# An attention kernel on Trainium2: the normalisation of the rows on ScalarE instead of VectorE

## The reference, cut to what matters

```
mod = (silu(c) @ wmod).reshape(8, 6, 1, 512)       # sa, ca, ga, sb, cb, gb
h = layernorm(x) * (1 + ca) + sa                    # x: 8 x 512 x 512, fp32
x = x + ga * attention(h, W_attn, W_proj)           # 16 heads of 32, causal
h = layernorm(x) * (1 + cb) + sb
x = x + gb * mlp(h)                                 # 512 -> 1024 -> 1024 -> 512
layernorm(x) = (x - mean(x)) / sqrt(var(x) + 1e-5)  # over the last axis
```

## Time and profile before

| | |
|---|---|
| median of 3 runs | 1541.73 us (1539.03 to 1541.76) |
| profiled execution, its own time | 1542.99 us |
| its span, first to last instruction | 1541.2 us |
| mean granted clock of TensorE | 0.973 of full |
| busy in the span: PE / DVE / ACT / POOL | 94% / 72% / 52% / 28% |

### The profile page before, as it was taken

How to read it: one execution, slowest core, us unless ns; L and a number is a source line. 1 busy time by engine, 2 the same in 40 slices (tenths; PEclk the granted TensorE clock), 3 DMA queues, 4 the chain that set the end, 5 groups by cost and what they waited for, 6 DMA issues and landing times.

```text
span 1541.2 us, 30440 instructions
## 1 busy us (share of the span) xinstructions
PE 1449.8 (94%) x12112; PEld 1314.9 (85%) x12112; DVE 1109.9 (72%) x1957; ACT 808.2 (52%) x1462; POOL 439.2 (28%) x451
## 2 busy tenths in 40 slices
PE   7989999999999999995599999998999999999998
PEld 6678878787888888874489999998999999999998
DVE  5377877777777877673577676787766666788887
ACT  3156666667666667674355555566333333353331
POOL 2146665667666766664000000000000000000000
PEclk9889999999999999997799999999999999999999
DMA  6634435244434343442434454363765556688895
GB/s 219 164 85 102 120 84 127 72 121 96 119 82 121 83 123 93 98 98 81 172 126 162 158 176 159 138 213 135 251 234 201 201 210 215 231 295 266 296 304 184
DMA packets 126590, 247.16 MB, mean 160 GB/s; under 512 B 13672, under 2 KB 36200, under 8 KB 126448
## 3 DMA queue, kind: packets, MB, share of 16 engines
q1 hardware_dynamic: 122816, 242.57, 50.5%
q10 hardware_dynamic: 3632, 2.64, 0.5%
HBM read 114.58 MB, written 79.72 MB: 126 GB/s over the span
## 4 chain that ended last, share of the span: by engine, by line
PE 45%; DVE 4%; ACT 2%; DMA 1%; issue 1%; SPq 0%; DVEq 0%; ACTq 0%
PE sum_b L2149 12%; PE sum_e L2149 8%; PE sum_a L2149 8%; PE aux L2089 6%; PE sum_b L2145 4%; PE sum_e L2145 3%; PE sum_a L2145 3%; PE aux L2099 1%; PE aux L2077 1%; DVE w L1841 1%; DVE op L1703 1%; DMA wproj_whole<-wproj_t 1%; ACT u_c L1443 0%; DMA y_dram<-u_c 0%; DMA blk<-y_dram 0%
## 5 line engine op out<-in xcount | busy, mean ns | idle before, releaser
L429 POOL TENSOR_TENSOR prob_lo<-prob,prob_hi 128x512 f16<-128x512 f32 x256 | 296.9, 1165 | 140.8 <-ACT prob L533 140.5
L526 ACT ACTIVATE prob_hi<-key_score 128x512 f16<-128x512 f32 x320 | 191.1, 597 | 130.6 <-PE key_score L824 128.2
L2149 PE MATMUL sum_b<-op,w 128*128 128x256 f32 x1728 | 217.9, 284 | 3.2 <-DVE p_c L1743 1.6
L735 PE MATMUL lin<-h_parts,wqkv 128*128 128x512 f32 x768 | 218.5, 408 | 1.1 <-DVE h_parts L578 1.1
L2149 PEld LDWEIGHTS sum_b<-op,w 128*128 128x128 f32 x1728 | 211.2, 192 | 5.4 <-issue 3.3
L533 ACT ACTIVATE prob<-key_score 128x512 f32<-128x512 f32 x320 | 190.7, 596 | 0.0
L697 DVE TENSOR_REDUCE row_max<-score 128x1 f32<-128x512 f32 (+2 forms) x384 | 180.4, 499 | 12.8 <-PE score L811 12.1
L735 PEld LDWEIGHTS lin<-h_parts,wqkv 128*128 128x128 f32 x768 | 143.0, 195 | 30.5 <-DVE h_parts L578 3.2
L811 PE MATMUL score<-stack 96*128 96x512 f32 (+3 forms) x512 | 155.2, 364 | 0.0
L2149 PE MATMUL sum_e<-op,w 128*128 128x256 f32 x1152 | 146.6, 284 | 3.7 <-DVE w L1841 2.3
L2149 PE MATMUL sum_a<-op,w 128*128 128x256 f32 x1152 | 145.4, 284 | 0.9 <-issue 0.9
(11 more groups left out here) (153 smaller groups left out, 2577.1 us busy)
## 6 DMA issues: line engine op xcount, KB each, us to landing
stack<-qk_parts SPq DMA_DIRECT2D x384, 128.0 KB, 2.4
late_op_whole<-y_dram SPq DMA_DIRECT2D x40, 512.0 KB, 4.9
y_dram<-u_c SPq DMA_DIRECT2D x32, 512.0 KB, 3.0
blk<-y_dram SPq DMA_DIRECT2D x32, 512.0 KB, 4.1
y_dram<-y_sum SPq DMA_DIRECT2D x24, 512.0 KB, 4.4
x_tiles<-x SPq DMA_DIRECT2D x32, 256.0 KB, 3.7
attn_dram<-o_rows SPq DMA_DIRECT2D x32, 256.0 KB, 2.3
attn_tiles<-attn_dram SPq DMA_DIRECT2D x8, 1024.0 KB, 6.1
```

The lines of the kernel that those rows point to most:

```text
L429: nc.gpsimd.tensor_tensor(prob_lo[:, key[1] % 2, u, :], prob[:, u, :], prob_hi[:, key[1] % 2, u, :], ALU.subtract).then_inc(lo_pool, 1)
L526: nc.scalar.activation(prob_hi[:, q % 2, u, :], bank[:], ACT.Exp, scale=SOFTMAX_SCALE, bias=P_SHIFT)
L735: mm = nc.tensor.matmul(lin_bank_of((QK, f))[:], wqkv[:, wl, c, at:at + P], h[:, hl, c, :], start=(c == 0 and k == 0), stop=(c == NC_ - 1 ...
L2149: mm = nc.tensor.matmul(dst, w[:, wl, c, cols], data[:, dl, c, :], start=begin, stop=end, skip_group_check=again)
```

## The change

ScalarE normalises, as x * rstd + shift, with shift = -mean * rstd. VectorE makes `shift` for the four tiles in one instruction in p2u3. The slots stay the same; on ScalarE too the instruction stands behind the other work of its unit. The first batch is still normalised by VectorE.

```
+    shift = mem.sb("shift", [P, NT])
...
+            def normalise(n, t):                                     # ScalarE
+                act.wait_ge(shift_ready, n)
+                nc.scalar.activation(xt[:, t, :], xt[:, t, :], ACT.Identity, scale=rstd[:, t:t + 1],
+                                     bias=shift[:, t:t + 1]).then_inc(x_norm, 1)
...
                     for n, item in work(b, p, u, more):
                         after_item(n, item)
+                    if more and (p, u) in NORM_AT:
+                        normalise(b + 1, NORM_AT.index((p, u)))
...
+            def minus_means(n):                                      # VectorE
+                dve.wait_ge(rstd_ready, n + 1)
+                dve.wait_ge(x_norm, NT * n)
+                nc.vector.scalar_tensor_tensor(out=shift[:], in0=mean_var[:, :, 0], scalar=-1.0, in1=rstd[:],
+                                               op0=ALU.mult, op1=ALU.mult).then_inc(shift_ready, 1)
...
-                    if more and (p, u) in NORM_AT:
-                        normalise(b + 1, (NORM_AT.index((p, u)),))
+                    if more and (p, u) == NORM_AT[0]:
+                        minus_means(b + 1)
```

More of the change, by code:

```diff
@@ L224, in attention @@
     x_in = [mem.sem(f"x_in{t}") for t in range(NT)]
-    aggr_done, var_ready, rstd_ready, x_norm, mod_ready = (
-        mem.sem(n) for n in ("aggr_done", "var_ready", "rstd_ready", "x_norm", "mod_ready"))
+    aggr_done, var_ready, rstd_ready, shift_ready, x_norm, mod_ready = (
+        mem.sem(n) for n in ("aggr_done", "var_ready", "rstd_ready", "shift_ready", "x_norm", "mod_ready"))
     lin_done, lin_act, lin_taken, h_low = (mem.sem(n) for n in ("lin_done", "lin_act", "lin_taken", "h_low"))
```

## The result

The changed kernel takes 1546.55 us (median of 8 runs, 1544.21 to 1549.17) against 1541.74 us for the kernel before (8 runs). The ratio is 1.0032, 95% interval 1.0021 to 1.0042: slower by 4.8 us, 3.2 to 6.5. I had forecast 1545.4 us, in a range of 1541.0 to 1550.0. One of the six executions of e8 took 1761.91 us at a mean granted clock of 0.746 and is left out of its median.

A forecast was written before the change was run, and what follows sets the result against it. TensorE's third turn was taken to wait on ScalarE's own sequence from p3u2 to `modulate`. Seven batches at 0.4 us (2.8) plus 0.9 us of clock, on 1541.73 us, gave 1545.4 us, range 1541.0 to 1550.0.

The forecast's parts named there:

- What sets the pace: ScalarE's sequence from p3u2 to `modulate` sets TensorE's third turn; most of VectorE's saving is hidden behind TensorE's work.
- Duration and hold of a normalisation: Each ScalarE normalisation takes 0.804 us, as L1382 does, and holds ScalarE for 0.7 us because neighbours overlap.
- `shift` in p2u3: In p2u3 ScalarE newly waits for VectorE's `shift`, held until GpSimd's L429 ends; exponentials of p2u4 1.0 us late.
- `shift` late: Rival: `shift` held by a whole L429, 1.3 us a batch, 9 us, 1551; chance 0.13 together with only the relief failing.
- p3u0, p3u1: ScalarE's gaps swallow nearly all the delay; the cast of p3u1 comes 0.15 us late.
- the relief at L680: Without L574 in p3u1, L680 of p3u2 and the DMAs behind it come 0.3 us earlier.
- my lower bound for this term: Third-turn delay over seven batches, forecast 2.8 us: at least 1.8 us, if p3u1's cast is not late.
- The clock: Falls of TensorE's clock behind longer third-turn gaps go from 2 to 2.5 at 1.8 us each: 0.9 us more.
- Sum: Third-turn delay of 2.8 us plus 0.9 us for the clock: 3.7 us slower, 1545.4 us.
- The signs I named: Signs of being wrong: normalisation hold other than 0.7 us, TensorE waiting in p3 for `prob`, `prob_lo` late for L844.

The follow-up runs named there:

- e8: Changed kernel with all four normalisations one place earlier (p2u2 to p3u1) and p4u2's two DMAs issued behind `modulate`: 1534.04 us, ratio 0.9948 to the kernel before.
- e1: Changed kernel with only the last tile (p3u3) normalised on ScalarE, the other three on VectorE: 1546.26 us, ratio 1.0040 to the kernel before.
- e2: Changed kernel with only the first three tiles (p2u3, p3u0, p3u1) normalised on ScalarE, p3u3's on VectorE: 1541.52 us, ratio 1.0000 to the kernel before.
- e4: Changed kernel with all four normalisations one place earlier (p2u2, p2u3, p3u0, p3u1): 1539.23 us, ratio 0.9988 to the kernel before.
- e7: Kernel before, with ScalarE's two DMAs of p4u2 issued behind the first `modulate`: 1534.07 us, ratio 0.9953.
- e3: Kernel before without L574, so no rows normalised from the second batch on, on either engine (output differs): 1537.57 us, ratio 0.9980.
- e6: Changed kernel with `shift` made in p2u2, nothing else moved: 1544.24 us, ratio 1.0021 to the kernel before.
- e5: Changed kernel run again, unaltered, beside other kernels: 1546.48 us against 1540.75 us for the kernel before, ratio 1.0035.
- e10: Changed kernel with 14 extra matmuls, results unused, on TensorE ahead of the third turn: 1542.50 us, ratio 1.0007 to the kernel before.
- e11: Only p3u3's tile normalised on ScalarE, plus 14 extra matmuls, results unused, ahead of the third turn: 1543.83 us, ratio 1.0016 to the kernel before.
- e9: Kernel before with 14 extra matmuls, results unused, on TensorE ahead of the third turn: 1538.35 us, ratio 0.9980.

## Why the prediction held, step by step

- **What sets the pace.** Right: ScalarE's own sequence from p3u2 to `modulate` sets the third turn (e1, e2, e4, e7); VectorE's 28 instructions were hidden (e3).
- **Duration and hold of a normalisation.** 0.82 us instead of 0.804, and 0.71 to 0.76 us of hold (257.73 to 258.45, 262.49 to 263.25, 267.37 to 268.08), near the 0.7 taken from L1382 and the neighbours' overlap.
- **`shift` in p2u3.** Right in place; it starts at once behind L596 and lasts 0.152 us, so that the rival "`shift` late" has nothing. I had made it wait for the rest of GpSimd's instruction. GpSimd was in L430 until 257.66, and L588 started ahead of that end and lasted no longer for it; so it is in all seven batches (151 to 154 ns, and 154 to 164 in e6, where GpSimd is idle then). The Trainium skill ("SBUF — State Buffer", "SBUF: two separate sides") has VectorE held there with two inputs in SBUF; here the trace doesn't agree, as far as an overlap of 0.12 us can tell.

```profile
256.50 1.16 POOL L430 TENSOR_TENSOR prob_lo<-prob,prob_hi 128x512 f16<-128x512 f32 x1 [2.28 <-ACT prob L539]
```
```profile
257.54 0.15 DVE L588 SCALAR_TENSOR_TENSOR shift<-mean_var,rstd 128x4 f32<-128x4 f32 x1
```

- **p3u0, p3u1: mis-sized.** I took the cast of p3u1 0.15 us late and the gaps not quite wide enough. In the steady batches the cast is on time, and the relief at L680 is the full 0.43 us, not 0.3: the third turn is 0.29 us later, not 0.4. That is near my lower bound for this term, 1.8 us in seven batches (0.25 each).
- **The batches are not alike: missed.** In the first one no weighted values stand before p3u1 (nothing is three pairs behind yet), TensorE is 0.8 us faster from p2u3 to p3u1, and ScalarE's gaps don't hold the load. Its third turn waits 2.6 us, 0.9 more than before. The trace of before shows it: from the L574 of p2u3 to that of p3u1 it is 98.96 - 94.02 = 4.94 us in the first batch and 261.33 - 255.62 = 5.71 in the batch of the earlier trace rows. The two lines of the first batch:

```profile
94.02 0.54 DVE L574 TENSOR_SCALAR x_tiles<-x_tiles,mean_var,rstd 128x512 f32<-128x512 f32 x1
...
98.96 0.54 DVE L574 TENSOR_SCALAR x_tiles<-x_tiles,mean_var,rstd 128x512 f32<-128x512 f32 x1
```

I had looked only at the wait, which was equal in all. e6 takes that extra away and nothing else. The two errors nearly cancel: 0.9 + 6 x 0.29 = 2.6 us, where I had 2.8. That this term came out so close is luck.
- **The clock: right in kind, sized loosely.** A fall costs 1.4 us (6.8 against 5.4 us), not 1.8; my value came from the length of a whole batch, which has other waits in it. The traces of the changed kernel have 3 and 4 falls against 2, so by the traces the term is about 1.5 x 1.4 = 2.1 us instead of 0.9; by the mean clock of the 12 runs of e5 it is 0.9 (above). Its size is not settled. That standing idle there brings the falls is shown by the filled kernels, e10 above all.
- **Sum.** 2.6 + 2.1 = 4.7 us, measured 4.8 and 5.7; with 0.9 us for the clock, 2.1 of the 5.7 us have no account.
- **The signs I named.** TensorE's waits for `prob` grow from 1.7 to 2.7 us, but none of them stands in p3; its one long wait for GpSimd's `prob_lo` (2.5 and 2.8 us) was there before. So neither sign of being wrong appeared.

By length of wait: 2 falls behind 41 third turns of up to 1.74 us, 12 behind the 22 of 1.9 to 2.6 us in the changed kernel (twice), e2 and e6. But e1, with the longest waits of all (2.4 us), has 1 in 7. So "the longer, the more often" doesn't hold throughout (e11's fall behind 1.74 us for row maxima is one more case), and with one trace for each kernel I can't tell chance from a cause such as where in time the waits lie. That stays open. So do the 1.6 us by which e10 minus e9 exceeds the 2.6 us of waits; they are inside the interval.

## What to carry to other kernels

In this kernel a move between two engines that both have slack cost or gave little but what it did at the one hand-over that the busy engine waits for, and the falls of the clock behind it. Find the sequence that ends last there, see which of the moved instructions lie in it, and give those another place: here four identical instructions cost 5 us, or gained 2 when each stood one place earlier and none was left in p3u3. And look at what the sequencer does ahead of a late instruction: two DMA issues in front of the one that everyone waits for were worth 6.7 us, 4.3 of it as shorter waits.

## What the runs showed of the hardware

- A wait of TensorE can cost more than its length. Filling seven waits of 1.7 us with matmuls that nobody needs made the kernel 3.4 us faster (0.9980, 0.9969 to 0.9991). The granted clock no longer fell to its lower level behind them (2 falls in the trace before, none after; mean clock 0.976 against 0.973). Not every wait does it: 2.4 us in e1 was followed by a fall once in seven.
- VectorE's small `shift` instruction (128x4, two inputs in SBUF) took 0.152 us although it started while GpSimd was still in L430, in seven of seven batches (for the last 0.12 us of it).
- A label in a trace can name the wrong engine: ScalarE's 0.52 us ahead of `modulate`, marked as a wait for TensorE, disappeared when its own two DMA issues of 0.63 us were moved behind it.
